# Routing's normalisation and gate products inside the second aggregation, node numbers in PSUM, quads weighed one time

## The reference

```python
x = x + gnn(layernorm(x))             # two GAT layers, 4 heads and 1 head, 50,000 edges, 3,125 nodes, 256 wide
x = x + ffn(layernorm(x))             # routed experts: 8 of them, top 1, capacity
x = x + hops(layernorm(x))            # 5 hops of a normalised adjacency, gated sum
x = x + slice_attention(layernorm(x))

# the end of a GAT layer, per destination node
out = segment_sum(hx[src] * al[:, :, None], dst)   # al: attention weights of the edges
# the head of ffn, on the layernormed x
logits = x @ gate_w + gate_b                       # (3125, 8)
probs  = softmax(logits);  idx = argmax(probs);  prb = probs[idx]
pos    = cumsum(one_hot(idx))[idx] - 1             # place within the expert, in order of rows
buf[idx, pos] = x                                  # where pos < capacity
```

## Time and profile before

| | us |
|---|---|
| median of 3 runs (lowest, highest) | 3929.01 (3926.93, 3930.06) |
| the profiled execution | 3929.17 |
| its span in the trace | 3927.4 |
| busy PE, DVE, ACT, POOL | 2784.9, 2073.5, 655.9, 1030.0 |
| DMA | 379.38 MB, mean 97 GB/s |

### The profile page before, as it was taken

How to read it: one execution, slowest core, us unless ns; L and a number is a source line. 1 busy time by engine, 2 the same in 40 slices (tenths; PEclk the granted TensorE clock), 3 DMA queues, 4 the chain that set the end, 5 groups by cost and what they waited for, 6 DMA issues and landing times. The chain is left out here.

```text
span 3927.4 us, 62644 instructions
## 1 busy us (share of the span) xinstructions
PE 2784.9 (71%) x16001; PEld 1820.9 (46%) x16126; DVE 2073.5 (53%) x4809; ACT 655.9 (17%) x1418; POOL 1030.0 (26%) x988
## 2 busy tenths in 40 slices
PE   5487746365766464488633995089999999996777
PEld 2244435234544352255423774056565656564445
DVE  6577659866854375466332003834444444443653
ACT  6455510041100001200001221300000000000321
POOL 0000017344777457677742001100000000000000
PEclk9799977687987676799875997599999999997887
DMA  3111145213444363355454332221313131312001
GB/s 139 23 42 42 43 163 185 77 52 90 119 114 110 107 201 111 105 152 160 140 166 180 111 119 92 97 97 56 105 56 107 56 105 56 107 59 72 0 10 36
DMA packets 206569, 379.38 MB, mean 97 GB/s; under 512 B 35808, under 2 KB 155345, under 8 KB 203223
## 3 DMA queue, kind: packets, MB, share of 16 engines
q1 hardware_dynamic: 117786, 181.72, 13.4%
q0 software_dynamic: 50384, 139.33, 12.5%
q10 hardware_dynamic: 38272, 56.91, 4.2%
HBM read 270.37 MB, written 108.29 MB: 96 GB/s over the span
## 5 line engine op out<-in xcount | busy, mean ns | idle before, releaser
L1982 PE MATMUL hop_wide<-hop_hs,counts 128*128 128x512 bf16 x3000 | 984.1, 380 | 0.0
L1984 PE MATMUL hop_narrow<-hop_hs,counts 128*128 128x256 bf16 x3125 | 853.0, 273 | 166.0 <-DMA hop_hs<-hop_parts 159.7
L656 POOL DMA_INDIRECT gat_ring<-hx_rows,src_i x784 | 831.9, 1061 | 324.6 <-issue 232.0
L1982 PEld LDWEIGHTS hop_wide<-hop_hs,counts 128*128 (+1 forms) x3125 | 306.2, 98 | 530.4 <-issue 162.8
L1363 PE MATMUL agg_acc<-agg_msg,agg_oh 128*128 x976 | 279.1, 439 | 124.7 <-DVE agg_oh L1297 124.4
L1363 PE MATMUL agg_acc<-gat_ring,agg_oh 128*128 x976 | 265.8, 416 | 83.2 <-DVE agg_oh L1294 78.8
L1984 PEld LDWEIGHTS hop_narrow<-hop_hs,counts 128*128 (+1 forms) x3125 | 306.2, 98 | 35.2
L1956 DVE TENSOR_SCALAR hop_h<-hop_narrow,all_dis 128x256 f32<-128x256 f32 x125 | 60.5, 484 | 481.2 <-PE hop_narrow L1984 476.6
L932 PE MATMUL cnt_acc<-cnt_oh 128*128 x1352 | 260.1, 336 | 64.4 <-issue 37.7
L847 DVE TENSOR_SCALAR cnt_oh<-cnt_number,cnt_column 128x1600 f16 x490 | 297.7, 639 | 8.3 <-issue 3.0
L1363 PEld LDWEIGHTS agg_acc<-agg_msg,agg_oh 128*128 128x128 f32 x976 | 198.3, 214 | 202.7 <-issue 170.0
(11 more groups left out here) (409 smaller groups left out, 3603.4 us busy)
## 6 DMA issues: line engine op xcount, KB each, us to landing
look_part<-src_low SPq DMA_DIRECT2D x28, 896.0 KB, 5.2
hop_hs<-hop_parts POOLq DMA_DIRECT2D x25, 960.0 KB
hop_parts<-hop_parts SPq DMA_DIRECT2D x125, 192.0 KB, 1.9
counts<-count_rows ACTq DMA_DIRECT2D x5, 4000.0 KB, 32.2
exp_w<-in_L_ffn_w SPq DMA_DIRECT2D x16, 1024.0 KB, 6.6
hop_acc<-x_gcn SPq DMA_DIRECT2D x125, 128.0 KB, 2.0
x_gcn<-hop_acc SPq DMA_DIRECT2D x125, 128.0 KB, 1.8
count_rows<-cnt_out SPq DMA_DIRECT2D x34, 400.0 KB, 2.3
```

Of the source, the lines that this page charges most:

```text
L656: pool.indirect_dma_start(out=self.ring[:, t % RING, :], out_offset=None, in_=self.g.hx_rows, in_offset=bass.IndirectOffsetOnAxis(ap=self. ...
L1982: pe.matmul(wide[bank][:, :], count, hs[:, t, 0:2 * D], start=(t == 0), stop=(t == NB - 1), skip_group_check=True)
L1984: return pe.matmul(narrow[bank], count, hs[:, t, 2 * D:3 * D], start=(t == 0), stop=(t == NB - 1), skip_group_check=True)
```

## The change

- edge_weights no longer makes g.nodes. ScalarE writes the 128 numbers of block b into a PSUM tile (number, two tiles in turn), and VectorE compares from there.
- In layer 0 a quad is multiplied by its weights one time; the second visit uses the msg of the first.
- In layer 1, class RouteRows does routing's work by block: VectorE takes the statistics of y behind each finish; after every fifth block the group of five gets its 1/sqrt and is scaled into xs. TensorE transposes block b - 7 at the start of block b and makes its gate products at the end; ScalarE copies the transpose and stores xs to x_route. y has eight buffers. The last seven blocks are done behind the last sum. Then gate_b is added to all logits.
- route loads x from x_route, with GpSimd's scatters waiting for the five parts, and begins with the logits. Its ScalarE issues the counts and then does the Exp.

The diff, cut to its core:

```diff
@@ -188,6 +188,8 @@
...
                 pool.memset(zero[:, :], 0.0).then_inc(filled, 1)
+                pool.iota(g.block_first[:, :], pattern=[[P, NB]], base=0, channel_multiplier=0,
@@ -1041,8 +1043,6 @@
...
             def _(pool):
-                pool.iota(g.nodes[:, :], pattern=[[1, NP]], base=0, channel_multiplier=0,
-                          allow_small_or_imprecise_dtypes=True)
@@ -1184,6 +1184,100 @@
...
+class RouteRows:
...
+    GROUP = 5
+    LAG = GROUP + 2
...
+    def load(self, eng, io):
+        eng.dma_start(self.gw[:, :, :], io["L0_ffn_gate_w"].rearrange("(p k) e -> p k e", p=P)).then_inc(self.given, 16)
+        eng.dma_start(self.gb[:, :], across(io["L0_ffn_gate_b"], NE)).then_inc(self.given, 16)
+    def stats_on_vector(self, dve, link, y, c):
+        dve.bn_stats(self.stats[:, c, :], y).then_inc(self.stat, 1)
+        if c % self.GROUP == self.GROUP - 1:
+            cols = self.group(c // self.GROUP)
+            dve.wait_ge(self.stat, after(c + 1))
+            for b in range(cols.start, cols.stop):
+                last = dve.bn_aggr(self.pair[:, b, :], self.stats[:, b, :])
+            link(last)
+            link(dve.tensor_scalar(self.var[:, cols], self.pair[:, cols, 1], LN_EPS, None, ALU.add))
+            dve.sem_inc(self.varied, 1)
+    def rows_on_vector(self, dve, link, y_of, k):
+        cols = self.group(k)
+        dve.wait_ge(self.rooted, after(k + 1))
+        inverse_root(dve, link, self.rstd[:, cols], self.var[:, cols], self.root[:, cols], self.half[:, cols])
+        for c in range(cols.start, cols.stop):
+            i = c % self.GROUP
+            if k:
+                dve.wait_ge(self.t_done, after(c - self.GROUP + 1))
+                dve.wait_ge(self.kept[i], after(16 * k))
+            dve.tensor_scalar(self.xs[i][:, :], y_of(c), self.pair[:, c, 0:1], self.rstd[:, c:c + 1], ALU.subtract,
+                              ALU.mult).then_inc(self.fed, 1)
+    def logits_on_vector(self, dve):
+        dve.wait_ge(self.given, after(32))
+        dve.wait_ge(self.m_done, after(NB))
+        dve.tensor_tensor(self.g.logits[:, :, :], self.lg[:, 0:NB * NE].rearrange("p (b e) -> p b e", e=NE),
+                          self.gb[:, :].unsqueeze(1).to_broadcast([P, NB, NE]), ALU.add)
+    def root_on_scalar(self, act, k):
+        cols = self.group(k)
+        act.wait_ge(self.varied, after(k + 1))
+        act.activation(self.root[:, cols], self.var[:, cols], ACT.Sqrt).then_inc(self.rooted, 1)
+    def copy_on_scalar(self, act, c):
+        act.wait_ge(self.t_done, after(c + 1))
+        if c >= 2:
+            act.wait_ge(self.m_done, after(c - 1))
+        act.activation(self.xt[c % 2][:, :, :].rearrange("p k n -> p (k n)"), self.turned[c % 2][:, 0:2 * P],
+                       ACT.Copy).then_inc(self.t_copied, 1)
+        act.wait_ge(self.fed, after(c + 1))
+        act.dma_start(self.g.x_route[c * P:(c + 1) * P, :], self.xs[c % self.GROUP][:, :]
...
+    def all_kept(self, act):
+        for i in range(self.GROUP):
+            act.wait_ge(self.kept[i], after(16 * len(range(i, NB, self.GROUP))))
+    def turn_on_tensor(self, pe, c):
+        pe.wait_ge(self.fed, after(c + 1))
+        if c >= 2:
+            pe.wait_ge(self.t_copied, after(c - 1))
+        for k in range(2):
+            mm = pe.transpose(self.turned[c % 2][:, k * P:(k + 1) * P], self.xs[c % self.GROUP][:, k:D:2],
+                              self.g.ident[:, :])
+        mm.then_inc(self.t_done, 1)
+    def gate_on_tensor(self, pe, c):
+        pe.wait_ge(self.t_copied, after(c + 1))
+        for k in range(2):
+            mm = pe.matmul(self.lg[:, c * NE:(c + 1) * NE], self.xt[c % 2][:, k, :], self.gw[:, k, :], start=(k == 0),
+                           stop=(k == 1), skip_group_check=True)
@@ -1202,12 +1296,19 @@
...
+        looped, inv = ([s.sb(f"{n}{i}", [P, w]) for i in range(2)] for n, w in (("looped", R), ("inv", H)))
+        YS = 8 if layer else 2
+        y = [s.sb(f"y{i}", [P, D]) for i in range(YS)]
+        rows = RouteRows(s, g) if layer else None
+        lag, group = RouteRows.LAG, RouteRows.GROUP
...
+        nodes = [s.ps(f"nodes{i}")[:, 0:P] for i in range(2)]
@@ -1229,6 +1330,8 @@
...
                 act.dma_start(bias[:, :], across(io[f"L0_gnn_bg{layer}"], D)).then_inc(consts, 16)
+                if layer:
+                    rows.load(act, io)
@@ -1245,26 +1348,45 @@
...
+                def number(b):
+                    if b >= 2:
+                        act.wait_ge(summed, after(b - 1))
+                    act.activation(nodes[b % 2], g.count[:, :], ACT.Identity, bias=g.block_first[:, b:b + 1]
+                                   ).then_inc(numbered, 1)
...
                 load(0)
+                number(0)
                 for b in range(NB):
                     make_self(b)
                     if b >= 2:
                         store(b - 2)
+                    if layer and b > group and b % group == 1:
+                        rows.root_on_scalar(act, b // group - 1)
                     if b + 1 < NB:
+                        number(b + 1)
                         if b >= 2:
                             act.wait_ge(self_made, after(H * (b - 1)))
                         load(b + 1)
+                    if layer and b >= lag:
+                        rows.copy_on_scalar(act, b - lag)
                 store(NB - 2)
+                if layer:
+                    rows.root_on_scalar(act, NB // group - 1)
                 store(NB - 1)
-                for i in range(2):
-                    act.wait_ge(stored[i], after(16 * TURNS[i]))
+                if layer:
+                    for c in range(NB - lag, NB):
+                        rows.copy_on_scalar(act, c)
+                    rows.all_kept(act)
+                for i in range(YS):
+                    act.wait_ge(stored[i], after(16 * len(range(i, NB, YS))))
@@ -1276,9 +1398,9 @@
...
+                    if not layer and (frees or not b):
                         weighted = dve.tensor_tensor(
-                            at(msg, (q + b) % 2).rearrange("p (k f) -> p k f", f=F + 1),
+                            at(msg, q % 2).rearrange("p (k f) -> p k f", f=F + 1),
@@ -1291,11 +1413,11 @@
...
-                                hot = dve.tensor_scalar(oh[k][:, n, :], g.nodes[:, row_of(b)], at(g.dst_f, tile),
+                                hot = dve.tensor_scalar(oh[k][:, n, :], nodes[b % 2], at(g.dst_f, tile),
                                                         at(g.w_cols, tile)[:, 0:1], ALU.is_equal, ALU.mult)
...
                             hot = dve.tensor_tensor(
-                                oh[k][:, :, :], g.nodes[:, row_of(b)].unsqueeze(1).to_broadcast([P, 2, P]),
+                                oh[k][:, :, :], nodes[b % 2].unsqueeze(1).to_broadcast([P, 2, P]),
@@ -1313,24 +1435,37 @@
...
+                def route_rows(c):
+                    rows_link = Linked(dve, rows.linked, linked_rows[0])
+                    rows.stats_on_vector(dve, rows_link, y[c % YS][:, :], c)
+                    if c >= group and c % group == 0:
+                        rows.rows_on_vector(dve, rows_link, lambda b: y[b % YS][:, :], c // group - 1)
+                    if c == NB - 1:
+                        rows.rows_on_vector(dve, rows_link, lambda b: y[b % YS][:, :], c // group)
+                        rows.logits_on_vector(dve)
+                    linked_rows[0] += rows_link.n
@@ -1339,13 +1474,20 @@
...
+                    if b and layer:
+                        route_rows(b - 1)
                     if b + 1 < NB:
+                        dve.wait_ge(numbered, after(b + 2))
                         first, last = last, visit(last, b + 1, False, lambda: last_quad(dve, b + 1))
                 finish(NB - 1)
+                if layer:
+                    route_rows(NB - 1)
@@ -1353,19 +1495,29 @@
...
+                    if layer and b >= lag:
+                        rows.turn_on_tensor(pe, b - lag)
...
-                        rows = at(ring, q % HELD) if layer else at(msg, (q + b) % 2)
+                        moving = at(ring, q % HELD) if layer else at(msg, q % 2)
...
+                    if layer and b >= lag:
+                        rows.gate_on_tensor(pe, b - lag)
                     first = last
+                if layer:
+                    rows.turn_on_tensor(pe, NB - lag)
+                    for c in range(NB - lag, NB):
+                        if c + 1 < NB:
+                            rows.turn_on_tensor(pe, c + 1)
+                        rows.gate_on_tensor(pe, c)
@@ -1396,30 +1548,19 @@
...
-        norm = Norm(s)
-        turned = [s.ps(f"turned{i}") for i in range(2)]
-        lg = [s.ps(f"lg{i}") for i in range(2)]
...
-                load_rows(sp, x, g.x_gnn, rows_came)
-                sp.dma_start(gw[:, :, :], io["L0_ffn_gate_w"].rearrange("(p k) e -> p k e", p=P)).then_inc(loaded, 16)
-                sp.dma_start(gb[:, :], across(io["L0_ffn_gate_b"], NE)).then_inc(loaded, 16)
```

(9 more changed lines are left out.)

107 lines of the change are left out of this document (42 added, 65 removed).

## The result

The changed kernel took 3876.92 us in the median of four runs (3875.66 to 3877.56), the kernel before 3929.53 (3926.93 to 3930.16): ratio 0.9864, 95% interval 0.9851 to 0.9876. The forecast was 3872, with 3858 to 3889 as its range. The profiled execution of the changed kernel took 3877.56 us (span 3876.0), 51.6 less than the one of before; 57.1 less were forecast.

What follows compares the result with a forecast made beforehand. GpSimd's gathers were taken to set the pace of both aggregations, with routing held by ScalarE's queue of counts. Terms -11 - 2 + 0.9 + 0 + 6.4 - 51.4 = -57.1 gave 3872 us from 3929.2, range 3858 to 3889.

Steps and rivals of the forecast that it cites:

- Part 1: First aggregation: 24 fewer multiplications stall GpSimd's gathers less, 0.47 us each, 11 us off; bounds 0 and 15.
- the tail: Behind the second aggregation's last sum: the last blocks' normalisation doesn't hide, 6.4 us on; bounds 3 and 15.
- the start: Start of the second aggregation: two more loads ahead of block 0 delay the first free slot 0.9 us; bounds 0.9 and 3.
- Part 2: Second edge weights: dropping GpSimd's 2.80 us iota of node numbers takes 2 us off; bounds 0 and 2.8.
- Part 3: Second aggregation: moved normalisation and gate products cost 0 beside the gathers, 6.4 us in the tail.
- Both hide: 0: Second aggregation: added VectorE (28 us) and TensorE (55 us) work hides behind GpSimd's gathers, costing 0.
- Part 4: Routing: 76.2 us remain against 127.6, with Exp behind 29.6 us of counts on ScalarE's queue; 51.4 us off.
- rival A: Routing: x rows come after the counts, so the end is 14 us later, 3886 us; chance 0.10.
- B: First aggregation gains nothing, as stalls move to other gathers or have another cause: 3883 us; chance 0.08.
- C: Second aggregation: new work only partly hidden, ring fills; 3932 us at worst, around 3900 if half seen; chance 0.07.
- D: Second aggregation: inserted waits bring TensorE's clock to 1.2 GHz, 583 us against the stage's 368, total 4090; chance 0.03.
- E: Tail behind the second aggregation: moved work isn't gone, 15 us instead of 6.4, total 3881; chance 0.07.

Runs made afterwards that it cites:

- the variant of the kernel before: Kernel before the change, with routing's five count transfers issued in experts 1 to 5 instead: 3908.9 us, ratio 0.9951.
- three reorderings: Changed kernel with Exp ahead of the counts, 3865.7 us; counts also behind the x rows, 3875.84; expert biases also loaded ahead of the counts, 3865.37.

## Why the prediction came out as it did

The direction, the order of the terms and the large one were right; the forecast was 5.7 us too low on the traces' own times. Terms worth 9.1 us erred to that side (part 1 4.7, the barrier 1.6, the tail 1.1, the start 0.8, the edge weights 0.65, others 0.25), and 3.4 to the other (the second gathers 1.6, routing 1.0, what follows 0.8). That the total came out within 6 us owes something to terms that cancel.

**Part 1, -11 against -6.3.** The step that failed is the mean: 57 us of stretched gathers shared out over 122 multiplications, 0.47 each. The run that puts the 24 back finds 0.30, and the mean gather stands at 1.145 us where the forecast's sign was 1.12. Gather by gather in the trace of before, what lies over 0.94 us in gathers that end with a multiplication comes to 60 us, but only 9.65 of them belong to second multiplications of a quad, 0.39 each. In the trace after, the 98 that stay have some 55 us, 0.56 each: part of the stalls only moved, as the bound of nothing had it. The value lay inside the bounds, in the lower half, where the forecast took the upper.

**Part 2.** -2 against -1.35 can't be judged: the same code gave 99.9 to 103.3 us for that stretch, and the variant of the kernel before, iota and all, 100.95. **The start, +0.9 against +1.7**, is right by the middle of its range (11.88 of nine traces, +1.0) and low for this trace: the last of block 0's loads is issued 0.80 us later behind the bias load, is waited for 0.55 longer and the visits up to the first freed slot take 0.33 more. The barrier ahead of it, +1.6, was in no term: the forecast put nothing for the new stage's semaphores, and the run with twenty more shows that GpSimd needs 0.08 us for each of them, 21 more than before, with the other engines waiting.

**Part 3.** "Both hide: 0" is shown by the doubled work (+0.7 us). For the one-hot tiles 0 was taken, and the gathers gained 1.6 us; with node numbers in SBUF they lose 2.6, so the gain is theirs, and the new work from SBUF took back at most 1.0. The tail was +6.4 by the sum, +7.5 by the trace. The term that failed is "transposes 0.8, copy 0.4": it lets five blocks through as if they were one. The last store is issued 9.0 us behind the start of the last sum, 8.5 later than before, since the blocks pass a round trip of TensorE and ScalarE at 1.17 us each. One microsecond was saved between the last store and routing (5.87 to 4.91); routing's stage has 17 semaphores where it had 33, and GpSimd arms them in 1.3 us instead of 2.5.

**Part 4, -51.4 against -52.4.** Its first term, 29.6 us of ScalarE's queue, came out as 27.68; the table load 1.28, as forecast; 7.8 to the first scatter measured 7.7; the last, 37.0, measured 38.1, by the one wait for x. The bound drawn from rival A, that x comes last, never bit: SP's issue of x took 24.05 us, in turn with the counts, and only scatter 20 was late.

**Rivals.** A, B and C fell: one scatter was 1.2 us late for x, the first aggregation did gain, and doubled work stayed hidden. D fell: the clock in the windows of the second aggregation is 0.97 to 1.00 up to 1961 and 0.77 only behind it, as these windows have it:

```profile
1811.00:1861.00 50.00, 43.45 (x185) 31.19 (x184) 36.02 (x105) 4.17 (x10) 37.82 (x41) 0.97 0.56 156
...
1911.00:1961.00 50.00, 34.97 (x155) 25.79 (x155) 29.36 (x88) 3.89 (x10) 37.81 (x41) 1.00 0.56 154
1961.00:2020.00 59.00, 45.67 (x159) 34.91 (x160) 30.49 (x90) 2.92 (x7) 39.98 (x42) 0.77 0.47 131
```

The kernel before had 0.77 already at 1900 to 1950. In D's working, and in C's, the 55 us of added TensorE work were read from routing, where the clock was 0.50; beside the gathers, at 0.97 to 1.00, 18 blocks took 19.9 us (11.5 and 8.4), 1.1 a block and not 2.2, so C's 83 us and D's 319, which take the 55 as work at the full clock, were too high (D's 583, at the low level, is not touched). E, a tail of 15 us, fell too: the tail is 1.1 us longer than listed, and 5 was its sign.

## What to carry to other kernels

Work moved beside an engine that sets the pace is free until that engine stops, so count the tail by itself: the last blocks go through one at a time, and each costs a full round trip, not its share of the busy time. Before a stage is shortened, look at what it had been hiding: a third of what was left of this one (26.4 of 75.2 us) went to five large loads that nobody needed there, and three reorderings only passed part of their cost on, until they were put under work that leaves the transfers idle. Of an interference that a trace shows as a mean over many instructions, removing some may bring back less than their share: here 0.30 us each instead of 0.47, since the rest met more of it. And measure a seam from the engine that arrives last at the barrier: a stage's semaphores cost 0.08 us each there, which a seam measured from another engine's last transfer hid.

## What the runs showed that was not expected

- A load of 32 KB in small packets took 2.6 us alone and 19.84 us beside a queue of large packets, at 1040 packets against 1180 in the same time. Its size didn't tell that; its number of packets did.
- ScalarE's queue stays closed while its large transfers are handed out: 21.5 us for five alone, 27.68 with x asked for in the same moment, 28.46 beside the scatters, and 35.07 with x asked for 1.4 us ahead of them.
- One-hot tiles made from PSUM take 405 ns and from SBUF 361, and yet the gathers beside the former are shorter, 953 ns instead of 962, and 2.6 us of the stage with them.
- Twenty-four multiplications from SBUF of 1.24 us cost the gathers beside them 7.1 us; doubling statistics and scalings, some 40 more VectorE instructions of 0.43 us, 0.7, which is within the range.
- Stretches with the same code differ between kernels by 1 to 4 us (the range column), more than three of the terms of the sum.
- A barrier ahead of a stage costs by the number of the stage's semaphores, 0.08 us each: 10.15 us with 16, 11.78 with 37, 13.35 with 57.
